# Attention block on one core: the second exponential ahead of the second tile's copies in ScalarE's order

## The chip, the cores and the metric

The kernel runs on one core of a Trainium2 chip. The metric is device time in microseconds (us) of one execution; the time before is the median of three runs.

## What is computed

Input x is 4 batches x 1024 tokens x 256. Three blocks follow one another: half of a feed-forward block with ternary weights is added to x, then attention, then half of the same feed-forward block again. The attention, cut to what matters (16 heads of 64, 4 memory keys ahead of the 1024, TOPK = 64):

```python
dots = einsum('bhid,bhjd->bhij', l2norm(q), l2norm(k)) * 10.0
dots = einsum('hg,bgij->bhij', W_pre_th, dots)          # mixes the heads
dots = where(causal, mask_value, dots)
vk   = top_k(dots, 64)[0][..., -1:]                     # the 64th largest of a row
dots = where(dots < vk, mask_value, dots)
attn = softmax(dots)
attn = einsum('hg,bgij->bhij', W_post_th, attn)         # mixes the heads again
out  = einsum('bhij,bhjd->bhid', attn, v)
```

then a gate, the output projection and the residual.

## The kernel before, in words

`build` runs `first_stage` (feed-forward and projections; its results go to DRAM), `attention` and `last_stage`. Only `attention` is touched.

Its unit is a **tile** g of 8 query rows x 16 heads, laid out as 128 partitions with the keys along the free axis. There are 512 tiles: 4 batches x 8 **query blocks** (`ib` 0 to 7, 128 rows each) x 16 tiles. A tile of block ib has `reach(g)` keys, from 12 to 1028, and ib + 1 **chunks** of 128 keys, its block's last tile one more (the 4 keys left over). Two tiles make a **pair** s: tiles 2s (even, the first) and 2s + 1 (odd, the second). There are 256 pairs.

Every engine's order is written out by hand in a loop over **steps** k; a tile passes through several steps:

- step s: TensorE mixes the heads of both tiles (`mix`, L1020 and L1024), VectorE takes the result into D (`take`, L1383).
- steps s to s + 2: the 64th largest is searched. ScalarE counts how many keys are over a guess (`count`, L1142, four rounds per tile: rounds 0, 1, 2, then 3 which writes SG), GpSimd moves the guess (L1217 to L1230) and prepares W (`signed`, L1252), VectorE picks the value (L1397, L1404, L1412).
- step s + 3: ScalarE writes the exponentials E (`exps`, L1152, one activation per tile), VectorE zeroes what is under the threshold and sums (`select`, L1462). E has four buffers, so `exps(g)` waits until TensorE has read tile g - 4 to the end (`act.wait_ge(s["post"], PC[g - 3])`). In the first four tiles of a batch it also waits for GpSimd's clearing of that buffer (`cleared`, L1279).
- step s + 4 for the even tile and s + 5 for the odd one: TensorE turns the weights and mixes the heads again (`post`, L1047), one product per chunk into PSUM banks 5 and 6 in turn, four chunks to a bank: a **group**. Blocks 0 to 3 have one group per tile (block 3's last tile two), blocks 4 to 7 two, and block 7's last tile, with nine chunks, three. A group whose bank was used two groups before waits for the copy out of it.
- step s + 5: ScalarE copies the groups out of PSUM into AT (`turned`, L1165; L1170 for the 4 keys left over), first the even tile's, then the odd one's.
- Every fourth step the values product of 8 tiles starts (`values`, L1075 and L1080, in four parts over three steps, into bank 7); its first part, in step k = 8 + 4 hb for the half block hb, waits until ScalarE has copied the odd tile of that same step.

In TensorE's order a step reads: mix of the even tile, values part 1, one piece of the next block's scores (`units`, L1006 and L1007), post of the odd tile of pair k - 5, mix of the odd tile, scores, values parts 3, 2 or 0, scores, the projection (L1089), post of the even tile of pair k - 4, scores. Every score piece is copied out by VectorE (L1372) before the next is written.

ScalarE's step is: round 3 of pair k - 2, `turned` of the even tile of pair k - 5, round 1 of pair k - 1, `exps` of the even tile of pair k - 3, `turned` of the odd tile of pair k - 5, `exps` of the odd tile of pair k - 3, round 2 of pair k - 1, round 0 of pair k. The two waits that meet here are these:

```python
            def exps(g):
                act.wait_ge(s["taken"], TC[g + 1])
                if g >= 4:
                    act.wait_ge(s["post"], PC[g - 3])
            def turned(g):
                for j, chunks in enumerate(turn_groups(g)):
                    i = PC[g] + j
                    act.wait_ge(s["post"], i + 1)
```

For `exps` of the odd tile g = 2(k - 3) + 1, tile g - 4 is 2(k - 5) + 1: the tile that `turned` copies in the same step. SyncE's order holds DMAs only.

Of the kernel before, what the change touches and what calls it, by code (L numbers as in the profile page):

```python
# [720 lines left out]
S = NT // 2  # L721
# [10 lines left out]
def reach(g):  # L732

    return MEM + R8 * (g % (IB * TPB) + 1)
# [22 lines left out]
def turn_groups(g):  # L757

    ib, t = g // TPB % IB, g % TPB
    chunks = list(range(ib + 2 if t == TPB - 1 else ib + 1))  # L760
    return [chunks[i:i + 4] for i in range(0, len(chunks), 4)]
# [25 lines left out]
def attention(nc, banks, mkT, kT_all, tail, qd, kd, gd, vd, x1d, x2d, sd, mix_rows, mem_v, Wo_d, delta_c,  # L787
# [16 lines left out]
    for G in range(NB):  # L804
        UC.append(UC[-1] + (len(score_units(G)) if G else 0))

    USED = [bank for g in range(NT) for _, bank in mix_plan(g)]
    LAST = [max([j for j in range(max(0, m - 4), m) if USED[j] == USED[m]], default=-1) for m in range(MC[NT])]

# [4 lines left out]
    def searched(p):  # L814

        return 0 <= p < S and 2 * p % (IB * TPB) >= FIRST
# [8 lines left out]
    with ExitStack() as ctx:  # L825
# [303 lines left out]
        @block.scalar  # L1129
        def _(act):  # L1130
            def count(g, r):
                e, n, i = g % 8, reach(g), 2 * FP[g // 2] + g % 2
                act.wait_ge(s[f"nt{r}"], FP[g // 2] + 1)
                if r == 3:
                    if i >= 2:
                        act.wait_ge(s["pick"], i - 1)
                    out = SG[:, g % 2, 0:n]
                else:
                    if r == 0 and i >= 2:
                        act.wait_ge(s["cnt2"], i - 1)  # L1140
                    out = junk[:, g % 2, 0:n]
                nc.scalar.activation(out, D[:, e, 1:1 + n], ACT.Sign, bias=nt[:, r, e:e + 1], scale=-1.0,  # L1142
                                     accum_out=cnt[:, r, e:e + 1]).then_inc(s[f"cnt{r}"], 1)

            def exps(g):
                e, n, t = g % 8, reach(g), g % (IB * TPB)
# [3 lines that stand above are left out]
                if t < 4:  # L1150
                    act.wait_ge(s["e_zero"], 4 * (g // (IB * TPB)) + t + 1)
                nc.scalar.activation(E[:, g % 4, 0:n], D[:, e, 1:1 + n], ACT.Exp, bias=least[:, e:e + 1],  # L1152
                                     scale=-1.0).then_inc(s["exp"], 1)

            def turned(g):
                ib, t, hb = g // TPB % IB, g % 8, g // 8
                if t % 4 == 0 and hb + t // 4 >= 2:
                    act.wait_ge(s["av"], hb - 1 + t // 4)
# [3 lines that stand above are left out]
                    bank, full = ps[5 + i % 2], [c for c in chunks if c <= ib]  # L1162
                    if full:
                        c0, c = full[0], len(full)
                        out = nc.scalar.activation(AT[:, c0:c0 + c, :, g % RING * R8:(g % RING + 1) * R8],  # L1165
                                                   bank[:, 0:c * P].rearrange("p (c h r) -> p c h r", h=H, r=R8),
                                                   ACT.Copy)
                    if len(full) < len(chunks):
                        c = (ib + 1) % 4
                        out = nc.scalar.activation(ATt[:], bank[0:MEM, c * P:(c + 1) * P].rearrange(  # L1170
                            "p (h r) -> p h r", h=H), ACT.Copy)
                    out.then_inc(s["at"], 1)

            act.wait_ge(s["sig"], 1)
            nc.scalar.activation(sigma[:], wvar[:], ACT.Sqrt, scale=QK_SCALE * QK_SCALE / DH).then_inc(s["sig"], 1)
            for k in range(S + 6):
                if searched(k - 2):
                    count(2 * (k - 2), 3)
                    count(2 * (k - 2) + 1, 3)
                if 0 <= k - 5 < S:  # L1180
                    turned(2 * (k - 5))
                if searched(k - 1):
                    count(2 * (k - 1), 1)
                    count(2 * (k - 1) + 1, 1)
                if 0 <= k - 3 < S:
                    exps(2 * (k - 3))
                if 0 <= k - 5 < S:
                    turned(2 * (k - 5) + 1)
                if 0 <= k - 3 < S:
                    exps(2 * (k - 3) + 1)  # L1190
                if searched(k - 1):
                    count(2 * (k - 1), 2)
                    count(2 * (k - 1) + 1, 2)
                if searched(k):
                    count(2 * k, 0)
                    count(2 * k + 1, 0)
# [639 lines left out]
```

## Time and profile before

| | |
|---|---|
| runs | median 3582.88 us of 3 (3573.04 to 3583.82) |
| the profiled execution | 3581.46 us, its span 3578.9 us |
| mean granted TensorE clock | 0.943 |
| busy | TensorE 88%, VectorE 71%, ScalarE 71%, GpSimd 56% of the span |
| attention | about 850 to 3290 us of the span |

A busy share is that of the whole span; the first and the last stage use ScalarE and VectorE little. "Idle before" in a row is the time in which the engine had nothing to do just ahead of the instruction, and behind the arrow stands what ended it. Stretches of attention are named here by batch (the first to the fourth) and query block.

### The profile page before, as it was taken

The page shows a single profiled execution, that of the slowest core. Times are in us where ns is not written, and L with a number is a line of the kernel's source. Part 1 is how long each engine was busy: PE and PEld are TensorE (multiplying, and loading weights), DVE is VectorE, ACT ScalarE, POOL GpSimd, SP SyncE. Part 2 cuts the span into 40 slices and gives each one's busy share as a digit, 9 for nine tenths or more (in the row PEclk, how much of TensorE's full clock was granted, in tenths as well). Part 3 has the DMA queues.
Part 4 walks back from the last instruction along what each step waited for, and adds up shares of the span by engine and source line. Part 5 has one row for each costly group of instructions (what it writes and reads, how often), then busy time and mean ns, then how long its engine had stood idle before and what let it go on. Part 6 is the DMA issues. An engine that isn't in the chain of part 4 may idle for free. (4 is left out here: it accounts for less than half of the span.)

```text
span 3578.9 us, 73640 instructions
## 1 busy us (share of the span) xinstructions
PE 3160.2 (88%) x23206; PEld 2089.0 (58%) x23206; DVE 2552.0 (71%) x6406; ACT 2523.4 (71%) x5857; POOL 2016.8 (56%) x6011
## 2 busy tenths in 40 slices
PE   7999999996788998888899887899988889988998
PEld 4444444443556666656666665566676566667566
DVE  4444444444788998678998867899986889986354
ACT  3444454443788999688999967889986888896222
POOL 1221221223787767687776767776777877674332
PEclk9999999996799999989999989999997999999899
DMA  3222222225466664355666345666534556642010
GB/s 129 94 90 104 106 106 94 83 82 173 141 179 179 185 181 98 108 155 173 185 183 157 90 119 151 179 179 186 144 88 130 166 178 181 181 108 74 12 36 30
DMA packets 363531, 467.11 MB, mean 131 GB/s; under 512 B 29476, under 2 KB 295204, under 8 KB 362664
## 3 DMA queue, kind: packets, MB, share of 16 engines
q1 hardware_dynamic: 363048, 461.62, 43.8%
q8 instruction: 187, 3.06, 0.4%
q14 instruction: 296, 2.42, 0.2%
HBM read 227.18 MB, written 234.36 MB: 129 GB/s over the span
## 5 line engine op out<-in xcount | busy, mean ns | idle before, releaser
L1142 ACT ACTIVATE junk<-D,nt 128x76 int8<-128x76 f32 (+62 forms) x1440 | 1070.4, 747 | 98.9 <-POOL nt L1230 65.2
L1047 PE MATMUL banks<-kr,E 128*128 128x128 f32 (+1 forms) x4672 | 707.0, 300 | 106.4 <-ACT AT L1165 60.7
L1047 PEld LDWEIGHTS banks<-kr,E 128*128 128x128 f32 (+1 forms) x4672 | 605.6, 203 | 256.7 <-issue 154.2
L1020 PE MATMUL banks<-Sg,kpre 128*128 128x109 f32 (+51 forms) x1568 | 605.1, 494 | 22.9 <-POOL maskb L1299 13.0
L1372 DVE COPY Sn<-banks 128x686 f32<-128x686 f32 (+11 forms) x440 | 375.5, 853 | 176.2 <-PE banks L1007 145.0
L1397 DVE SCALAR_TENSOR_TENSOR W<-SG,sgn,W 128x76 f32<-128x76 int8 (+14 forms) x480 | 412.8, 899 | 103.4 <-POOL W L1252 102.9
L1006 PE MATMUL banks<-kT,qT 64*128 64x343 f32 (+11 forms) x880 | 395.8, 532 | 101.9 <-DVE Sn L1372 95.9
L1165 ACT ACTIVATE AT<-banks 128x512 f32<-128x512 f32 (+3 forms) x768 | 345.2, 479 | 195.6 <-PE banks L1047 194.5
L1075 PE MATMUL banks<-AT,V 128*64 128x64 f32 x9216 | 394.1, 233 | 87.6 <-issue 75.4
L1075 PEld LDWEIGHTS banks<-AT,V 128*64 128x64 f32 x9216 | 324.2, 143 | 162.6 <-issue 143.1
L1462 DVE SCALAR_TENSOR_TENSOR E<-D,vk,E 128x12 f32<-128x12 f32 (+56 forms) x512 | 394.8, 780 | 3.1 <-ACT E L1152 1.5
L1007 PE MATMUL banks<-kT,qT 64*128 64x343 f32 (+11 forms) x880 | 396.2, 533 | 0.0
L1142 ACT ACTIVATE SG<-D,nt 128x76 int8<-128x76 f32 (+14 forms) x480 | 357.1, 746 | 49.1 <-DVE hit L1412 46.2
L1152 ACT ACTIVATE E<-D,least 128x12 f32<-128x12 f32 (+56 forms) x512 | 369.4, 722 | 9.6 <-POOL E L1279 6.5
L1252 POOL TENSOR_SCALAR W<-D,sgn 128x76 f32<-128x76 f32 (+14 forms) x480 | 375.5, 792 | 0.4
L1383 DVE TENSOR_SCALAR_CACHE_REDUCE D<-banks 128x13 f32<-128x13 f32 (+62 forms) x504 | 339.1, 673 | 41.3 <-PE banks L1024 40.9
L1020 PEld LDWEIGHTS banks<-Sg,kpre 128*128 128x128 f32 x1568 | 267.5, 205 | 169.6 <-issue 114.5
L1404 DVE MAX8 m<-W 128x8 f32<-128x76 f32 (+14 forms) x480 | 326.7, 720 | 22.1 <-issue 19.9
L541 POOL TENSOR_TENSOR a_g2T<-a_gT 128x512 f32<-128x512 f32 x64 | 70.7, 1109 | 460.3 <-ACT a_gT L455 460.3
L1229 POOL TENSOR_TENSOR move<-cnt,tab 128x2 f32<-128x2 f32 x720 | 223.7, 311 | 188.2 <-ACT junk L1142 183.5
L1142 ACT ACTIVATION_READ_ACCUMULATOR junk<-D,nt 128x1 f32 x1440 | 276.0, 192 | 0.0
L1230 POOL TENSOR_TENSOR nt<-move,base 128x2 f32<-128x2 f32 x720 | 224.7, 312 | 56.4
(197 smaller groups left out, 5253.9 us busy)
## 6 DMA issues: line engine op xcount, KB each, us to landing
score_scratch<-Sn SPq DMA_DIRECT2D x96, 343.0 KB, 3.3
v_scratch<-a_share SPq DMA_DIRECT2D x32, 512.0 KB, 3.6
q_scratch<-a_share SPq DMA_DIRECT2D x32, 512.0 KB, 2.8
k_scratch<-a_share SPq DMA_DIRECT2D x32, 512.0 KB, 2.8
gate_scratch<-a_share SPq DMA_DIRECT2D x32, 512.0 KB, 2.7
kT<-k_scratch SPq DMA_DIRECT2D x32, 512.0 KB, 5.0
gateT<-gate_scratch SPq DMA_DIRECT2D x32, 512.0 KB, 10.2
qT<-q_scratch SPq DMA_DIRECT2D x31, 512.0 KB, 6.4
```

What stands on the lines that cost most here:

```text
L1006: nc.tensor.matmul(ps[0][:, 0:c1 - c0], qT[0:DH, p, :], kT[0:DH, p, c0:c1], start=True, stop=True)
L1007: nc.tensor.matmul(ps[1][:, 0:c1 - c0], qT[DH:P, p, :], kT[DH:P, p, c0:c1], start=True, stop=True).then_inc(s["s_ps"], 1)
L1020: out = nc.tensor.matmul(bank[:, 0:c], kpre[:].rearrange("p h r -> p (h r)"), Sg[:, g % 3, c0:c1], start=True, stop=not diagonal)
L1047: out = nc.tensor.matmul(ps[5 + i % 2][0:rows, c % 4 * P:(c % 4 + 1) * P], E[:, g % 4, c * P:c * P + rows], kr[:, g % 4, :], start=True, s ...
L1075: out = nc.tensor.matmul(into, V[:, c, h * DH:(h + 1) * DH], rows, start=(c == 0), stop=(c == ib and (ib > 0 or hb % 2 == 0)))
L1142: nc.scalar.activation(out, D[:, e, 1:1 + n], ACT.Sign, bias=nt[:, r, e:e + 1], scale=-1.0, accum_out=cnt[:, r, e:e + 1]).then_inc(s[f"cnt ...
L1152: nc.scalar.activation(E[:, g % 4, 0:n], D[:, e, 1:1 + n], ACT.Exp, bias=least[:, e:e + 1], scale=-1.0).then_inc(s["exp"], 1)
L1165: out = nc.scalar.activation(AT[:, c0:c0 + c, :, g % RING * R8:(g % RING + 1) * R8], bank[:, 0:c * P].rearrange("p (c h r) -> p c h r", h= ...
L1252: ts(W[:, g % 2, 0:n], D[:, g % 8, 1:1 + n], sgn[:, g % 8:g % 8 + 1], -SMALL, ALU.mult, ALU.mult).then_inc(s["v"], 1)
L1372: nc.vector.tensor_copy(Sn[:, i % 2, :, 0:c1 - c0], banks[:, 0:2, 0:c1 - c0]).then_inc(s["s_sb"], 1)
L1397: nc.vector.scalar_tensor_tensor(out=W[:, h, 0:n], in0=SG[:, h, 0:n], scalar=sgn[:, e:e + 1], in1=W[:, h, 0:n], op0=ALU.is_equal, op1=ALU. ...
L1462: nc.vector.scalar_tensor_tensor(out=E[:, g % 4, 0:n], in0=D[:, g % 8, 1:1 + n], scalar=vk[:, g % 8:g % 8 + 1], in1=E[:, g % 4, 0:n], op0= ...
```

## The change

```diff
@@ -1184,10 +1184,13 @@
                 if 0 <= k - 3 < S:
                     exps(2 * (k - 3))
-                if 0 <= k - 5 < S:
+                full = 0 <= k - 5 < S and len(turn_groups(2 * (k - 5) + 1)) > 2
+                if full:
                     turned(2 * (k - 5) + 1)
                 if 0 <= k - 3 < S:
                     exps(2 * (k - 3) + 1)
+                if 0 <= k - 5 < S and not full:
+                    turned(2 * (k - 5) + 1)
                 if searched(k - 1):
                     count(2 * (k - 1), 2)
```

In ScalarE's step the copies of the odd tile of pair k - 5 stand behind the exponential of the odd tile of pair k - 3. A tile of more than two groups (nine chunks, the last of a batch) keeps its old place: its third group is written into the bank of its first, so TensorE can't end it before ScalarE has copied, and the exponential waits for that end. No other engine's order is touched.

ScalarE, query block 5, from the exponentials of tile 8 of the block (684 keys) on; `AT<-banks` is one group's copy, with 4 x 16 and 2 x 16 head columns of 8 rows:

```order
 L1152 ACTIVATE E<-D,least 128x684
-L1165 ACTIVATE AT<-banks 128x64x8
-L1165 ACTIVATE AT<-banks 128x32x8
 L1152 ACTIVATE E<-D,least 128x692
+L1165 ACTIVATE AT<-banks 128x64x8
+L1165 ACTIVATE AT<-banks 128x32x8
 L1142 ACTIVATE junk,cnt<-D,nt 128x716
 L1142 ACTIVATE junk,cnt<-D,nt 128x724
```

The second exponential has moved ahead of both groups' copies; the counts stay behind them all.

ScalarE at the end of a batch, where block 7's tiles (two groups of four chunks each) are copied between the exponentials of the next batch's first tiles:

```order
 L1152 ACTIVATE E<-D,least 128x12
-L1165 ACTIVATE AT<-banks 128x64x8 x2
 L1152 ACTIVATE E<-D,least 128x20
-L1165 ACTIVATE AT<-banks 128x64x8 x2
+L1165 ACTIVATE AT<-banks 128x64x8 x4
 L1152 ACTIVATE E<-D,least 128x28
 L1165 ACTIVATE AT<-banks 128x64x8 x2
```

The odd tile's two copies have moved behind the exponential of 20 keys and now stand right ahead of the next even tile's two. Behind the exponential of 28 keys stand copies of the tile of nine chunks, which have not moved.

## Rows read from the trace of the kernel before

**Rows 1.** The page: busy time of each engine over the span.

```profile
PE 3160.2 (88%) x23206; PEld 2089.0 (58%) x23206; DVE 2552.0 (71%) x6406; ACT 2523.4 (71%) x5857; POOL 2016.8 (56%) x6011
```

**Rows 2.** Windows, third batch, blocks 4 to 6 (PE, PEld, DVE, ACT, POOL, PEclk, DMA, GB/s).

```profile
2314.00:2397.00 83.00, 74.88 (x663) 53.30 (x663) 75.11 (x179) 73.89 (x177) 60.77 (x193) 0.96 0.61 177
2397.00:2488.00 91.00, 84.34 (x764) 57.50 (x763) 84.99 (x179) 83.76 (x178) 64.70 (x194) 0.98 0.66 187
2488.00:2587.00 99.00, 90.24 (x861) 64.74 (x860) 89.49 (x179) 93.16 (x178) 67.92 (x193) 0.97 0.60 154
```

**Rows 3.** Waits of the whole span: total us, times, longest.

```profile
ACT AT L1165 <- PE banks L1047: 194.5, 149, 5.3
...
PEld banks L1047 <- DVE E L1462: 86.1, 70, 3.9
```

**Rows 4.** Who waited for the exponentials of line 1152, whole span.

```profile
  DVE E L1462: 1.5, 3
```

**Rows 5.** Timeline, third batch, block 5, ScalarE and TensorE (start, us, what, idle before).

```profile
2419.13 0.86 ACT L1152 ACTIVATE E<-D,least 128x684 f32<-128x684 f32 x1
2421.95 0.87 ACT L1165 ACTIVATE AT<-banks 128x512 f32<-128x512 f32 x2 [1.96 <-PE banks L1047]
2422.71 0.87 ACT L1152 ACTIVATE E<-D,least 128x692 f32<-128x692 f32 x1
...
2420.76 1.60 PE L1047 MATMUL banks<-kr,E 128*128 128x128 f32 x12
...
2426.67 1.60 PE L1047 MATMUL banks<-kr,E 128*128 128x128 f32 x12
```

**Rows 6.** Timeline, VectorE: the select of the second of those exponentials.

```profile
2430.54 0.98 DVE L1462 SCALAR_TENSOR_TENSOR E<-D,vk,E 128x692 f32<-128x692 f32 x1
```

**Rows 7.** Timeline, third batch, block 6, the same place.

```profile
2516.73 1.16 ACT L1165 ACTIVATE AT<-banks 128x512 f32<-128x512 f32 x2 [2.19 <-PE banks L1047]
...
2515.53 1.83 PE L1047 MATMUL banks<-kr,E 128*128 128x128 f32 x14
```

**Rows 8.** Windows behind such places, columns as in rows 2.

```profile
2335.00:2363.00 28.00, 25.87 (x208) 20.55 (x207) 25.54 (x66) 26.73 (x66) 21.04 (x69) 0.94 0.66 175
2424.00:2464.00 40.00, 36.25 (x357) 26.52 (x356) 37.91 (x83) 39.52 (x85) 31.03 (x90) 1.00 0.67 180
2519.00:2599.00 80.00, 70.83 (x669) 52.78 (x669) 72.94 (x148) 79.27 (x149) 59.52 (x161) 0.96 0.55 133
2371.00:2421.00 50.00, 46.58 (x413) 30.91 (x414) 45.41 (x98) 42.48 (x96) 35.13 (x105) 0.95 0.57 179
2661.00:2678.00 17.00, 15.39 (x224) 13.46 (x223) 13.32 (x33) 8.71 (x12) 9.37 (x16) 1.00 0.22 64
```

**Rows 9.** Timeline, third batch, block 7: first part of the values product and what follows.

```profile
2651.72 1.06 ACT L1165 ACTIVATE AT<-banks 128x512 f32<-128x512 f32 x2
2652.67 1.12 ACT L1152 ACTIVATE E<-D,least 128x996 f32<-128x996 f32 x1
...
2652.83 2.08 PE L1075 MATMUL banks<-AT,V 128*64 128x64 f32 x64 [0.21 <-ACT AT L1165]
...
2654.85 1.38 PE L1047 MATMUL banks<-kr,E 128*128 128x128 f32 x10
...
2659.87 1.05 ACT L1165 ACTIVATE AT<-banks 128x512 f32<-128x512 f32 x2
```

**Rows 10.** Timeline, start of the fourth batch, ScalarE, GpSimd and TensorE.

```profile
2679.93 0.60 ACT L1165 ACTIVATE AT<-banks 128x512 f32<-128x512 f32 x1 [0.30 <-PE banks L1047]
2681.03 0.31 ACT L1152 ACTIVATE E<-D,least 128x20 f32<-128x20 f32 x1 [0.50 <-POOL E L1279]
...
2679.96 0.95 POOL L1279 MEMSET E<- 128x1028 f32 x1 [1.94 <-PE banks L1047]
...
2681.36 0.91 PE L1047 MATMUL banks<-kr,E 128*128 128x128 f32 x6 [0.64 <-issue]
```

**Rows 11.** Window around rows 9, columns as in rows 2.

```profile
2645.00:2660.00 15.00, 12.50 (x187) 11.27 (x186) 12.36 (x30) 13.37 (x25) 11.54 (x25) 0.89 0.35 87
```

## The prediction, made before the changed kernel ran

> **What bounds the kernel.** I read the page first: TensorE is busy 88% of the span, VectorE and ScalarE 71% each [rows 1]. That average hides the attention, so I cut its third batch by query block [rows 2]. In blocks 4, 5 and 6 ScalarE is busy 89, 92 and 94%, VectorE 90, 93 and 90%, TensorE 90, 93 and 91%. Three engines are nearly full at once and each waits for the others in turn, so a delay on one may reach the end, and a wait taken off one is mostly replaced by another. Then I asked who waits at the two operations that change places. ScalarE sits idle ahead of copies for 194.5 us in 149 waits, always until TensorE's post is done [rows 3]. VectorE, the only reader of an exponential, waits for it 1.5 us in the whole run [rows 4].
>
> **What is moved.** 252 of the 256 odd tiles have at most two groups; for the last of them, pair 254, no exponential is left, so 251 times an exponential goes ahead of copies. No instruction is added or dropped, and no DMA or other queue is passed. Three things can change.
>
> *(a) The exponential is ready earlier.* It moves ahead by one tile's copies, 0.87 us in block 5. The one at 2422.71 ends at 2423.58 and is selected at 2430.54 [rows 5, 6]: it had 7 us to spare. So what the change brings forward is not waited for. The gain is bounded by the 1.5 us of rows 4; I take 0.5.
>
> *(b) ScalarE's wait is the same wait, and it gets longer.* The odd copies wait for post of tile 2(k - 5) + 1; the odd exponential waits for the end of post of that same tile, for it writes the buffer E of four tiles on. It can't run while the copies would have waited. But the first copy waits only for the first group, and the exponential for the last. Rows 5 show it: post starts at 2420.76, 12 matmuls in 1.60 us, of which 8 are the first group; the copy starts at 2421.95, beside the second group's four, then comes the exponential. Afterwards the exponential starts at about 2422.40 and both copies follow it, so ScalarE is later by the second group's time, or by one copy (0.6 us) if that is less. The price by block: post takes 1.60 us for 12 matmuls and 1.83 for 14 [rows 5, 7], or about 0.22 us for each chunk's two matmuls. The second group has one chunk in block 4 (0.22 us), two in block 5 (0.45), three in block 6 (0.67, so 0.6), four in block 7 (0.6); the last tile of blocks 4 and 5 has a chunk more (0.54 and 0.6). In blocks 0 to 3 there is one group and the loss is nil (block 3's last tile aside).
>
> It is paid only where ScalarE stands waiting at the odd copy. Going through the timeline, that is three tiles of block 4 in every batch (0.22, 0.22, 0.54), three of block 5 (0.45, 0.45, 0.6), one of block 6 (0.6) and two of block 7 (0.6 each): 4.3 us a batch, **17 us in four**. Not all of it reaches the end. Behind the first such place of block 4, ScalarE is busy 26.7 of 28 us; behind that of block 5, 39.5 of 40; behind that of block 6, 79.3 of 80 [rows 8]. It does not catch up there, so 0.22 + 0.45 + 0.6, 5 us in four batches, goes through in full. Around the other places of blocks 4 and 5 it is busy 42.5 of 50 us and TensorE 46.6 [rows 8]: ScalarE would wait again anyway. Of those 7 us I take a third, 2.5. In block 7 the two places lie where TensorE is busy 15.4 of 17 us and ScalarE 8.7 [rows 8]: nothing. Term (b): **+7.5**, bounds 0 and 17.
>
> *(c) The copies land later, by one exponential (0.4 to 1.1 us).* TensorE needs them twice. Post of the next even tile reuses their bank. In rows 5 both copies end at 2422.82 and that post starts at 2426.67, 3.9 us later; in blocks 1 to 7 the timeline shows nowhere less than the exponential's length. Covered. If that cover went, each of 128 two-group tiles would cost up to 1.1 us less the slack. The exception is the start of batches 2 to 4: there the odd exponential also waits for GpSimd to clear E, which starts when post ends (2679.96), so the exponential starts at 2681.03 in either order [rows 10]; the copies would then run from about 2681.35 to 2682.5, and post of the next tile, which starts at 2681.36, waits until 2681.95. That is 0.6 us three times, where TensorE and ScalarE feed each other directly: **+1.8**.
>
> The second reader is the first part of the values product, once in four steps. In blocks 0 to 5 it starts behind the copies by more than the exponential lasts, or waits for something later. In blocks 6 and 7 it comes at once: in rows 9 the copies end at 2652.78 and the product starts at 2652.83 after 0.21 us idle. Nine such places in blocks 6 and 7 would wait 0.15 to 1.1 us longer, about 7 us in all. But TensorE runs ahead there: the post behind that product starts at 2654.85 and takes 2 us, while ScalarE collects it at 2659.87 [rows 9], 3 us late. I take 0; what covers it is ScalarE's being full, and if TensorE were the bound, it would cost the 7 us.
>
> Sum: 7.5 + 1.8 - 0.5 = about +9 us. On the profiled execution's 3581.5 us that is 3590.5; this execution stands 1.4 us under the median of 3582.9. I say **3591**, which is 0.2% over the median. A measurement of this kernel tells about 0.3% from no change, that is 3572 to 3593.6.
>
> **Rivals.** *B, slower: a longer TensorE stall that isn't absorbed.* The mechanism is the wait of the values product's first part in blocks 6 and 7. It decides as soon as TensorE's lead there (3 us) is gone, for instance because (b) has already made all three engines late together. Then all of (b) and (c) goes through: 17 + 7 + 1.8 = 26 us, 3608. For it: three engines at 90% and more leave little to absorb with. Against it: the lead of rows 9. A longer stall may cost clock on top. The window around rows 9 has a granted clock of 0.89 [rows 11], so 0.22 of its 15 us, 3.3 us, ran at the lower level of 1.2 GHz while TensorE had been idle 2.5 us of it. One more such stretch at each of the nine places costs up to half of 3.3 us times TensorE's busy share of 0.83, 1.4 us, or 12 us in all: 3620. The Trainium skill (TensorE: Matmul & The Clock Gate, Part 1) says that the throttled clock is the default and that only activity releases it; by that rule each longer wait of TensorE may add one such stretch, and the upper figure would be the sum. The trace agrees so far as the clock is lowest where TensorE idles (0.89 against 0.98 in block 5), but it doesn't show how near these places are to another fall. 23%.
>
> *C, nothing happens.* All of (b) is absorbed, since wherever ScalarE waits TensorE is late, and it may be late again at the next wait. 3581 to 3583. For it: 149 waits spread over all blocks. Against it: ScalarE's full stretches in rows 8. 15%.
>
> *D, faster: the earlier exponentials do help.* TensorE's weight loads wait 86.1 us for selects [rows 3]. If a tenth of that hung on an exponential behind copies, the time would be 3572. For it only that VectorE's idle time is not always given a releaser; against it rows 4 and 6, and VectorE's order, in which select stands far behind. A different interleaving of three full engines may also fall out well, or leave the clock up in more places. 12%.
>
> *E, the change does not do what it says.* The order of ScalarE's instructions shows the exchange at 251 places; I leave this no chance.
>
> **How the numbers follow.** The forecast has 50%, spread from 3583 to 3597 (its terms' bounds without the values product), of which 36 points lie under 3593.6 and 14 over. B's 23 are slower; C's 15 are no change; D's 12 give 9 faster and 3 no change. Faster 0.09, no change 0.54, slower 0.37. The range leaves out most of D and the clock part of B: 3576 to 3611.
>
> **What would show it.** Right: the idle time ahead of line 1165's odd copies moves to the exponentials of line 1152, whose sum with line 1165's idle grows by 10 to 17 us over 195 + 10; VectorE's wait for exponentials stays under 2 us; post (L1047) finds its copies as before, except at the batch starts; TensorE's wait at L1075 for copies grows by about 7 us in blocks 6 and 7 with no longer steps around it. Wrong towards B: steps of blocks 6 and 7 longer by 0.5 us and more, and a mean clock under 0.94. Wrong towards C: the summed idle of ScalarE unchanged. Wrong towards D: TensorE's waits for selects shorter by several us, or blocks 0 to 3, where I expect no change at all, shorter. If those four blocks move by over 2 us in total, my reading of what the copies are waited for is wrong.

## The result: slower by 0.5%

Twenty runs of each kernel: the changed one has a median of 3587.9 us (3579.5 to 3595.8), the one before 3571.6 us (3553.2 to 3583.8). The ratio is 1.0049 with a 95% interval of 1.0036 to 1.0062, so the change costs 13 to 22 us. Two of the three runs of before that stood ahead of the prediction, and its profiled execution, were among the slowest of their kernel; with twenty, its median is 11 us lower. The profiled execution of the changed kernel took 3591.5 us, its span is 3588.9 us, and the mean granted clock is 0.943 as before.

The page of the changed kernel, part 1, against rows 1:

```profile
span 3588.9 us, 73640 instructions
...
PE 3156.3 (88%) x23206; PEld 2085.6 (58%) x23206; DVE 2555.8 (71%) x6406; ACT 2520.9 (70%) x5857; POOL 2024.4 (56%) x6011
```

Every engine has the same number of instructions. TensorE and ScalarE are busy 4 and 2.5 us less, VectorE and GpSimd 4 and 8 us more, in one execution each. At ScalarE, what has grown is idle time. The groups of ScalarE by line, over the whole span of the changed kernel (busy us, mean ns, idle time before them and who ended it):

```profile
L1152 ACT ACTIVATE E<-D,least 128x12 f32<-128x12 f32 (+56 forms) x512 | 356.3, 723 | 152.5 <-PE banks L1047 134.0 <-POOL E L1282 12.8 <-DVE D L1386 4.9
L1165 ACT ACTIVATE AT<-banks 128x512 f32<-128x512 f32 (+3 forms) x768 | 340.7, 476 | 77.5 <-PE banks L1047 77.5
```

Before, the copies stood behind 194.5 us of waits for post [rows 3] and the exponentials hardly waited. Now 134.0 us of it stand ahead of the exponentials and 77.5 ahead of the copies: 73 of the even tiles, 4 of the nine-chunk tiles, which keep their order. Both lines together sat idle 205.2 us before and 230.0 after: 25 us more, of which 17 are waits for post (194.5 against 134.0 + 77.5) and 6 are waits for GpSimd's clearing of E at the starts of the batches. Who waited for the exponentials is as it was in rows 4, here the answer for the changed kernel's line 1152:

```profile
who waited for it (us, times):
  DVE E L1465: 1.5, 3
```

The earlier exponentials brought VectorE nothing.

The place of rows 5 in the changed kernel's timeline (ScalarE, then TensorE):

```profile
2432.76 0.87 ACT L1152 ACTIVATE E<-D,least 128x692 f32<-128x692 f32 x1 [2.47 <-PE banks L1047]
2433.54 0.85 ACT L1165 ACTIVATE AT<-banks 128x512 f32<-128x512 f32 x2
...
2431.06 1.60 PE L1047 MATMUL banks<-kr,E 128*128 128x128 f32 x12
```

Post takes the same 1.60 us. ScalarE waits 2.47 us for its end where it waited 1.96 us for its first group, and the first copy, which ran beside the second group, now comes behind it and behind the exponential.

### The profile page after: what moved, and what is told of

It is laid out like the page before. It is cut to its first block and busy times, and to the rows that moved or that the text cites. A ratio compares the mean times of both kernels' runs of the same rounds, so it can differ in the third digit from the quotient of the medians.

```text
span 3588.9 us, 73640 instructions
## 1 busy us (share of the span) xinstructions
PE 3156.3 (88%) x23206; PEld 2085.6 (58%) x23206; DVE 2555.8 (71%) x6406; ACT 2520.9 (70%) x5857; POOL 2024.4 (56%) x6011
## 5 line engine op out<-in xcount | busy, mean ns | idle before, releaser
L1142 ACT ACTIVATE junk<-D,nt 128x76 int8<-128x76 f32 (+62 forms) x1440 | 1070.2, 747 | 96.3 <-POOL nt L1233 65.1
L1047 PE MATMUL banks<-kr,E 128*128 128x128 f32 (+1 forms) x4672 | 704.5, 299 | 110.6 <-ACT AT L1165 72.7
L1152 ACT ACTIVATE E<-D,least 128x12 f32<-128x12 f32 (+56 forms) x512 | 356.3, 723 | 152.5 <-PE banks L1047 134.0
L1165 ACT ACTIVATE AT<-banks 128x512 f32<-128x512 f32 (+3 forms) x768 | 340.7, 476 | 77.5 <-PE banks L1047 77.5
L1233 POOL TENSOR_TENSOR nt<-move,base 128x2 f32<-128x2 f32 x720 | 229.5, 319 | 56.4
```

Of the source, the lines that this page charges most:

```text
L1047: out = nc.tensor.matmul(ps[5 + i % 2][0:rows, c % 4 * P:(c % 4 + 1) * P], E[:, g % 4, c * P:c * P + rows], kr[:, g % 4, :], start=True, s ...
```

## The experiments

### The parts of the change, each alone

Four kernels ran with 28 runs of before on the same chip.

**e1** exchanges only at tiles of one group:

```diff
-                full = 0 <= k - 5 < S and len(turn_groups(2 * (k - 5) + 1)) > 2
+                full = 0 <= k - 5 < S and len(turn_groups(2 * (k - 5) + 1)) > 1
```

> The exchange only at odd tiles of one group (query blocks 0 to 3, but for block 3's last tile); all others keep the order of before. The whole change cost 16 us (0.46%). Theory W (ScalarE's wait gets longer by the second group's post): one-group tiles have nothing to lose, so this equals before within 2 us. Rival L (the copies land later, and TensorE's next readers wait, in all blocks): the changed kernel's trace has the first batch's blocks 0 to 3 longer by 5.7 us, so 5 to 8 us over before.

Measured: 3570.7 against 3569.9 us, ratio 1.0006 (0.9993 to 1.0018). Nothing that can be measured (-2 to +6 us), as theory W says. The stretch that made rival L is no more than the spread of single executions: from the first post of the first batch to the first of its block 4 the changed kernel's trace is 4.5 us longer than that of before, but over all four batches blocks 0 to 3 differ by 2.0 us.

**e2** exchanges only at tiles of two groups (the condition ends in `!= 2`).

> The exchange only at odd tiles of two groups (blocks 4 to 7 and block 3's last tile). Theory W: all of the 16 us is here, +13 to +17 us. Rival L: only about half, +6 to +11 us. ScalarE's idle time ahead of lines 1152 and 1165 together, 205 us before and 230 after the change, should be 225 to 230 by W.

Measured: 3585.4 us, ratio 1.0034 (1.0016 to 1.0051), or 12 us by the ratio and 15 by the medians. All or most of the cost is in the tiles of two groups.

**e3** leaves the order as it was and only makes the first copy wait for the whole of post:

```diff
                 ib, t, hb = g // TPB % IB, g % 8, g // 8
...
+                if g % 2 and len(turn_groups(g)) == 2:
+                    act.wait_ge(s["post"], PC[g + 1])
                 for j, chunks in enumerate(turn_groups(g)):
```

> The order of before, but the first copy of an odd tile with two groups waits until post has ended the second group too: the longer wait alone, with nothing landing behind an exponential. Theory W: as e2, +12 to +17 us. Rival V (the values product's first part finds its copies late in blocks 6 and 7): +3 to +8 us, since only part of the wait passes through and V's part is missing.

Measured: 3581.3 us, ratio 1.0034 (1.0022 to 1.0046), 8 to 16 us. That is e2's cost without moving a single instruction.

**e4** splits the copies around the exponential (`turned` with a second argument copies that group alone):

```diff
+                split = 0 <= k - 5 < S and len(turn_groups(2 * (k - 5) + 1)) == 2
                 if 0 <= k - 5 < S:
-                    turned(2 * (k - 5) + 1)
+                    turned(2 * (k - 5) + 1, 0 if split else None)
                 if 0 <= k - 3 < S:
                     exps(2 * (k - 3) + 1)
+                if split:
+                    turned(2 * (k - 5) + 1, 1)
```

> In odd tiles of two groups the first group's copy stays ahead of the exponential and only the second group's goes behind it; one-group tiles as before. ScalarE's wait is not longer than before, but the last copy lands one exponential later, as in the change. Theory W: within 3 us of before. Rival V (late copies hold up the values product): +6 to +10 us. If both parts count, e3 and e4 add up to e2.

Measured: 3567.8 us, ratio 1.0000 (0.9982 to 1.0018). The exponential goes ahead of the last copy, that copy lands later, and nothing is lost that these runs can measure (-6 to +6 us), while the first copy keeps its place beside the second group's products. So the cost is in the main the wait (b), and not the landing (c); e3 and e4 together give e2.

### How much of the wait passes through

> The longer wait alone (as in e3, order of before), only in blocks 4 and 5, where the prediction counted 10 us at ScalarE and let 5 of them pass. e3 cost 12 us in all. Theory A (a small term passes in full wherever ScalarE waits, in blocks 4 and 5 above all, because everything behind it waits for ScalarE again): +8 to +11 us, nearly e3. Rival S (shares as predicted, the rest elsewhere): +4 to +6 us.

The edit is e3's with `and ib in (4, 5)`. Measured: 3575.5 against 3569.7 us, ratio 1.0013 (0.9996 to 1.0029), -1 to +10 us.

> The same only in blocks 6 and 7, where 7 us were counted at ScalarE and 2.4 let pass. Theory A: +2 to +4 us. Rival V (block 7 is not absorbed): +6 to +8 us.

The same with `and ib in (6, 7)`. Measured: 3573.6 us, ratio 1.0009 (0.9995 to 1.0023), -2 to +8 us.

The two sum to about 8 us where e3 gave 12; within their intervals they agree. e5's 4.6 us is at the predicted share and under theory A, but its interval holds both. These runs don't settle the shares block by block.

### Is it paid only where ScalarE stands waiting?

**e7** takes away what makes the odd tile's post late. In TensorE's order:

```diff
-                if k >= 9 and (k - 9) % 4 == 0 and (k - 9) // 4 < 2 * NB:
-                    values((k - 9) // 4, 1)
                 units(G, slots[0])
                 if 0 <= k - 5 < S:
                     post(2 * (k - 5) + 1)
+                if k >= 9 and (k - 9) % 4 == 0 and (k - 9) // 4 < 2 * NB:
+                    values((k - 9) // 4, 1)
```

> ScalarE's order of before; in TensorE's order part 1 of the values product, which comes once in four steps just ahead of the odd tile's post, goes behind it. All the places where ScalarE waits for the odd tile's post in blocks 4 to 7 lie in such steps (1.4 to 2.2 us each). Theory P (that part is what makes the odd post late): ScalarE's idle time ahead of odd copies in blocks 4 to 6 falls from 45 us to under 15, and the time falls by 5 to 25 us. Rival T (TensorE is as full as ScalarE, so whatever is put off comes back as a wait at the next even tile): idle only moves, time within 4 us of before.

> e7 with the change's ScalarE order. The change costs only where ScalarE stands waiting for the odd post, so if e7 takes those waits away the exchange costs little on top of it: e8 over e7 by 0 to 5 us instead of 16. Rival L (the copies' landing one exponential later is what costs): e8 over e7 by 12 us or more.

Measured: e7 3585.5 us, ratio 1.0043 (1.0028 to 1.0057); e8 3585.6 us, ratio 1.0042 (1.0026 to 1.0057). Two readings. First, on e7's order the exchange costs nothing that can be measured (0.1 us by the medians, within 8 us either way by the two intervals), where on the order of before it cost 16: the same 251 copies land one exponential later in e8, so on this order landing late is not the cost. e8 does not show the absence of the wait, though. In its trace ScalarE waits 147.5 us for post (82.4 ahead of copies, 65.1 ahead of exponentials) where e7's has 119.3, a growth of 28 us against 17 in the changed kernel, and the end doesn't move: a longer sum of waits is not by itself a longer time. Second, e7 itself is a miss: I expected a gain or nothing and it is slower by 15 us. Waits of e7, attention stage (total us, times, longest):

```profile
ACT AT L1165 <- PE banks L1047: 119.3, 120, 4.5
PEld banks L1047 <- DVE E L1462: 115.4, 111, 3.9
ACT junk L1142 <- POOL nt L1217: 85.2, 103, 13.7
...
DVE flag L1379 <- PE banks L1034: 73.8, 71, 3.5
```

ScalarE's wait for post fell by 75 us from rows 3, as meant. In its place ScalarE waits 85.2 us for the first guess, which was 30.3 us before, TensorE's post waits 115.4 us for selects against 86.1 [rows 3], and VectorE waits 73.8 us for the odd tile's mix, now behind the values product, against 20.4. The idle time came back in other places, with a loss; which of them makes the 15 us was not followed further.

**e12** makes the change's exchange only in steps with k % 4 other than 1:

```diff
-                full = 0 <= k - 5 < S and len(turn_groups(2 * (k - 5) + 1)) > 2
+                full = 0 <= k - 5 < S and (k % 4 == 1 or len(turn_groups(2 * (k - 5) + 1)) > 2)
```

> The change's exchange only in the steps without part 1 of the values product (k % 4 other than 1): three quarters of the odd tiles, all the places where the values product's first part reads the copies, but only 14 of the 35 waits at odd tiles of two groups (block 7's and those of the last pairs of blocks 4 and 5), where the prediction let little pass. Theory W: +1 to +7 us over before, well under the change's 16. Rival L or V (copies that land one exponential later cost by themselves): three quarters of the change or more, +12 us and over.

Measured: 3573.0 against 3574.3 us, ratio 1.0003 (0.9989 to 1.0016). Three quarters of the exchanges, among them every one that the values product's first part waits for, cost nothing that can be measured (-4 to +6 us). By difference, 16 us less this, some 10 to 23 us, the cost sits in the quarter where part 1 of the values product stands ahead of the odd post and ScalarE waits. No run makes the exchange in that quarter alone on the order of before.

### Taking the wait off the exponential

If the exponential cost time only since it waits for the very post that the copies wait for, it should gain time once it needn't. A fifth buffer for E does that: `exps(g)` then waits for tile g - 5, the even tile before. To make room for it in SBUF, these three kernels leave out the 4 leftover V rows of block 7 and use the memory's rows in their place.

```diff
-        E = sb("E", [P, 4, JW])
+        E = sb("E", [P, NE, JW])
...
-                if g >= 4:
-                    act.wait_ge(s["post"], PC[g - 3])
-                if t < 4:
-                    act.wait_ge(s["e_zero"], 4 * (g // (IB * TPB)) + t + 1)
+                if g >= NE:
+                    act.wait_ge(s["post"], PC[g - NE + 1])
+                if t < NE:
+                    act.wait_ge(s["e_zero"], NE * (g // (IB * TPB)) + t + 1)
```

with `NE = 5` and the clearing adapted. e10 has `exps` of the odd tile ahead of `turned` in every step, e11 only where k % 4 is 1.

> Order of before, but E has five buffers, so that an odd exponential waits for post of the even tile before (tile g - 5), not for the tile that is being copied. To make room this kernel leaves out the 4 leftover V rows of block 7: the last keys of each batch's last tile are weighted with the memory's rows instead (all instructions stay but for one small DMA per batch, split from another). In this order the copies wait for that post anyway, so every theory expects the time of before within 4 us. It is the base for e10 and e11.

> e9 with all odd exponentials ahead of the odd tile's copies (nine-chunk tiles too). Theory W: the exchange cost time because the exponential waited for the same post to its end; freed of that wait it runs inside ScalarE's idle time ahead of odd copies. In the trace of before 81 odd copies were waited for, and an exponential in each gap would fill 47 us; with a third to all of it passing through this is faster than e9 by 15 to 40 us. Rival L (copies that land one exponential later are what costs): slower than e9 by 10 us or more, since 170 copies that were not waited for land later. Rival F (three full engines: filled idle time comes back elsewhere, as in e7): within 5 us of e9.

> e9 with the exchange only in the steps that hold part 1 of the values product (k % 4 == 1), where 53 of the 81 waits lie and ScalarE waits longest. Same room made in the same way as in e9. Theory W: most of e10's gain, 8 to 30 us under e9, and if landing late costs anything at all, more than e10. Rival F: within 5 us of e9.

Measured, against 3572.2 us for before: e9 3577.3 us, ratio 1.0007 (0.9988 to 1.0026); e10 3563.7 us, ratio 0.9982 (0.9967 to 0.9996); e11 3564.1 us, ratio 0.9981 (0.9967 to 0.9995). The buffer alone does nothing that can be measured. With it the exchange that cost 16 us gains about 9 us against e9 by the ratios (some 0 to 18, the two intervals combined), and 6 (1 to 12) against before. Its size is below what I expected (15 us and more for e10), its sign is theory W's. e11 gains what e10 does, within 7 us either way: no help or harm of the other three quarters can be seen.

The place of rows 5 in e10 (its lines are six further down; the two exponentials stand in one row):

```profile
2406.80 1.62 ACT L1158 ACTIVATE E<-D,least 128x684 f32<-128x684 f32 x2
2409.62 0.87 ACT L1171 ACTIVATE AT<-banks 128x512 f32<-128x512 f32 x2 [1.20 <-PE banks L1053]
...
2408.42 1.60 PE L1053 MATMUL banks<-kr,E 128*128 128x128 f32 x12
```

Both exponentials are done by the time post starts, ScalarE waits 1.20 us instead of 1.96, and the first copy starts 1.20 us behind the start of post, as in rows 5, with the second group still running. Over attention, ScalarE's wait for post is 205.6 us in e9 and 145.1 in e10:

```profile
ACT AT L1171 <- PE banks L1053: 145.1, 130, 4.1
```

So the two traces differ by 60 us of idle time, and the two kernels by some 9 us.

### How much of this could be the clock

The runs scatter, and they scatter with the granted clock. Over the 106 runs of before that e1 to e12 were compared with, the time is 1.6 us longer for each 0.001 by which the run's mean granted clock is lower (correlation -0.67); which of the two causes the other is not shown. The mean clock of the changed kernel's twenty runs is 0.9435 against 0.9443 for those 106, which would be 1 us of its 16. For the differences of a few us it matters more. With one slope fitted over all runs (1.9 us for 0.001), the differences from before at equal clock are these estimates, each with an interval of 3 to 4 us either way: e3 11.5 us, e2 13.1, e1 3.0, e4 2.1, e12 4.0, e7 15.0, e8 13.7, e9 0.4, e10 -5.2, e11 -5.7, and e10 against e9 -5.6. The order of the findings stays: the wait alone costs, the split order costs little, and with a fifth buffer the exchange gains. But e12's three quarters may cost some 4 us, and the gain over e9 may be nearer 6 than 9; if it is the change that moves the clock, the figures without this correction are the right ones.

## Why the prediction was right or wrong

**The sign and the place: right.** I forecast a loss, and put it down to (b), the exponential waiting for the end of the post whose first group is enough for the first copy. e3 gives most of that cost without any exchange, e4 makes the exchange without that wait and costs nothing measurable, and e10 turns the sign by taking the wait off.

**The size: the term (b) was too small.** It said +7.5 us of bounds 0 to 17. e3 measures 12 us (8 to 16) and e2, which is (b) with late landing, 12 (6 to 18); the whole change costs 16 (13 to 22). With it the class was wrong too: I gave "no change" 54% and slower 37%, and it was slower. The time was inside the range.

The step of (b) that failed is "It is paid only where ScalarE stands waiting at the odd copy". There is a second kind of place: ScalarE arrives when the first group is done and the second is not. Before, the first copy didn't wait there, so my list of waited-for copies left these places out. The odd tile five pairs behind that of rows 5, in the kernel before (ScalarE, then TensorE):

```profile
2477.08 0.87 ACT L1165 ACTIVATE AT<-banks 128x512 f32<-128x512 f32 x2
2477.83 0.94 ACT L1152 ACTIVATE E<-D,least 128x772 f32<-128x772 f32 x1
...
2475.88 1.60 PE L1047 MATMUL banks<-kr,E 128*128 128x128 f32 x12
```

and in the changed one:

```profile
2489.77 0.94 ACT L1152 ACTIVATE E<-D,least 128x772 f32<-128x772 f32 x1 [0.46 <-PE banks L1047]
2490.61 0.85 ACT L1165 ACTIVATE AT<-banks 128x512 f32<-128x512 f32 x2
...
2488.07 1.60 PE L1047 MATMUL banks<-kr,E 128*128 128x128 f32 x12
```

Post runs until 2477.48 and the copy starts at 2477.08, unhindered; now the exponential waits 0.46 us. In block 5 this happens at two tiles of every batch, 0.46 and 0.48 us. These two show the mechanism but not the cost: they lie in steps with k % 4 of 2 and 3, and e12 has them as well, here the same tile in its trace:

```profile
2471.24 0.94 ACT L1152 ACTIVATE E<-D,least 128x772 f32<-128x772 f32 x1 [0.52 <-PE banks L1047]
```

The place of that kind in the quarter that e12 leaves alone is tile 9 of block 7 (counted from 0, as above), in every batch. Third batch, before:

```profile
2661.85 0.58 ACT L1165 ACTIVATE AT<-banks 128x512 f32<-128x512 f32 x1
2662.65 0.60 ACT L1165 ACTIVATE AT<-banks 128x512 f32<-128x512 f32 x1 [0.22 <-PE banks L1047]
...
2660.59 2.02 PE L1047 MATMUL banks<-kr,E 128*128 128x128 f32 x16 [0.69 <-ACT AT L1165]
```

and changed:

```profile
2676.19 1.14 ACT L1152 ACTIVATE E<-D,least 128x1012 f32<-128x1012 f32 x1 [0.98 <-PE banks L1047]
2677.24 1.06 ACT L1165 ACTIVATE AT<-banks 128x512 f32<-128x512 f32 x2
...
2674.04 2.05 PE L1047 MATMUL banks<-kr,E 128*128 128x128 f32 x16
```

ScalarE's waits for the odd tile's post in blocks 4 to 7, added up tile by tile from the three traces, and what I had counted (us):

| | before | changed | e12 | growth counted |
|---|---|---|---|---|
| steps with k % 4 = 1 | 38.6 | 56.4 | 37.6 | 7.8 |
| the other steps | 16.0 | 22.7 | 22.8 | 9.4 |

The other steps' waits grew by 6.7 us in both kernels, and e12 says that this costs nothing measurable. In the steps that matter they grew by 17.8 us, more than twice my count: in block 4 by 2.8 us (counted 1.8), in block 5 by 3.5 (3.6), in block 6 by 5.6 (2.4) and in block 7 by 5.8 (0). So the count was right for block 5 and failed in blocks 6 and 7, where tile 9 of block 7 waits for 1.0 to 2.4 us instead of 0.2 to 0.6, and where other tiles wait now that did not before: tile 1 of block 7 in three batches, and tile 9 of block 6 in two, by up to 2.04 us. At that last one ScalarE came 1.2 us behind the whole post before (third batch), so it is not a second group's price but a consequence of the engines' changed timing. Even if all of the 7.8 us had passed, it would be less than the 10 to 23 us that e12 leaves to these steps; at equal clock these steps have some 11 us, so that gap is not sure. Over all blocks the idle time ahead of both lines grew by 25 us, where I had forecast 10 to 17.

**What passes through.** I let 44% of (b) pass. 16 us of end time over 25 us of more idle time is about two thirds. My argument "ScalarE would wait again anyway" for the places followed by partly idle stretches is borne out by e12 for the last pairs of blocks 4, 5 and 7: there the exchange cost nothing measurable. It was too hopeful for the rest, if the growth there is what costs. How the shares lie between the blocks stays open (e5 and e6), and so does why 28 us of longer waits for post from e7 to e8 cost nothing.

**(a), no gain: right.** VectorE waits 1.5 us for exponentials, as before.

**(c), late landing.** That the bank's reuse is covered held: no post of an even tile waits for a copy in either trace. The sign that I gave, "post finds its copies as before", did not: post's waits for copies grew from 60.7 us in 39 to 72.7 us in 38. All of them are at odd tiles, and what they wait for is the even tile's copy, which was not exchanged; it comes late because ScalarE does. e12's trace has 72.5 us of them at no measurable cost, so their growth is not the loss either. For the batch starts I said +1.8 us, because post of the next tile would wait 0.6 us for the copies. ScalarE's waits for the cleared buffer did grow, from 6.5 us in 12 waits to 12.8, but the post behind them didn't wait for copies; the changed kernel's TensorE at the place of rows 10:

```profile
2695.23 2.02 PE L1047 MATMUL banks<-kr,E 128*128 128x128 f32 x16 [1.25 <-DVE E L1465]
```

It waited for a select. No run isolates the batch starts. e12 makes the same exchange there (12.8 us of waits for the cleared buffer in its trace too) and costs nothing measurable, so the 1.8 us are neither shown nor excluded. The values product's waits for copies grew more than I said, from 18.7 to 39.8 us at line 1075 with weight loads and matmuls counted separately, here the changed kernel's line 1075:

```profile
its engine sat idle before it (us, times) until:
  issue: 212.7, 147
  ACT AT L1165: 22.8, 14
  ACT ATt L1170: 17.0, 31
```

Counted once, by the weight loads, it is 11.2 us before and 26.6 after. Of that 9.9 us are 20 new waits of 0.34 to 0.66 us in blocks 1 to 5, where I had written that the product starts late enough; before there was none. That such waits would be absorbed held: e12 keeps every one of those exchanges, with 29.9 us of waits, at no measurable cost.

**The rivals.** B had the right sign and the whole change's time nearly (3608 on the profiled execution's base is +26; measured +16), but for the wrong reason in part: its deciding mechanism, a values product that isn't absorbed, was priced at 7 us, and e4 and e12, which have it, measure 0 (-6 to +6) and 1 (-4 to +6), while its share of 1 for (b) is nearer than my 0.44. Its sign, steps of blocks 6 and 7 longer by 0.5 us, didn't come either: block 6's 32 steps are longer by 0.16 us on average in the changed kernel's trace, block 7's by 0.03. Nor did its added clock loss: the mean clock is 0.943 in both traces, and 0.97 in the third batch's block 6 and 0.94 in its block 7 in both. Single waits of TensorE at the values product grew by about 1 us there, the one of rows 9 from 0.21 to 1.23. The Trainium skill (TensorE: Matmul & The Clock Gate, Part 1) says that the default state is throttled and that activity releases it; no cost of that kind shows in these traces. C and D didn't happen.

**The base.** I forecast 3591 us from a profiled execution that, as it turned out, was 10 us over its kernel's median. The absolute time came out near (3587.9) because two errors of opposite sign met: a base 10 us too high and a sum some 7 us too small (+9 for a measured +16). That part is luck. The spread given for the forecast's own terms was also added up too short: with (b) at 17 it reaches 3600, not 3597.

## What to carry to other kernels

When two instructions of one engine wait for the same producer, look at how much of the producer each needs: the one that is content with its first part goes first, and an exchange can cost the time of the rest, also at places where the first copy doesn't wait in the trace. Count those places too, and ask an experiment which of them the end time hangs on: here the most regular of them cost nothing measurable. Before moving an instruction forward to fill a wait, read what it waits for itself; if it is the same event, no order of the two fills the wait, and a further buffer has to come first (here the same exchange went from +16 us to some -6 to -9 us). And in a kernel whose engines are all 90% busy, a sum of idle time from one trace gives the sign and the place but not the time: 25 us added went with 16 us, 60 us filled with about 9, and 28 us more from e7 to e8 with nothing. Give a three-run median no more trust than its spread.

## What was not expected of the hardware

The scatter of single executions of this kernel, on one core with the same data, is larger than the effects sought: twenty runs of before spread over 30.6 us (0.86%), and part of this goes with the mean granted clock of the run, which lay between 0.936 and 0.951 for the same kernel. A single trace's blocks differ by 5 us too where the program is the same (block 1, its four batches together, is 5.2 us shorter in e2's trace than in that of before, with no instruction moved in it). Reading a sub-part's cost from one trace against one trace is not possible here below some 5 us.
